# First attention of a two-layer network: three rounded products become one unrounded product, and the score tiles change their order

## The reference

```python
def _L0_xattn_ref(x, latents, ln_m_g, ln_m_b, ln_l_g, ln_l_b, Wq, Wkv, Wout):
    heads, dim_head = (16, 64)
    scale = dim_head ** (-0.5)
    x = layer_norm(x, ln_m_g, ln_m_b)
    lat = layer_norm(latents, ln_l_g, ln_l_b)
    q = lat @ Wq
    kv_input = jnp.concatenate([x, lat], axis=1)
    kv = kv_input @ Wkv
    k, v = jnp.split(kv, 2, axis=-1)
    ...
    dots = jnp.einsum('bhid,bhjd->bhij', q, k) * scale
    attn = jax.nn.softmax(dots, axis=-1)
    out = jnp.einsum('bhij,bhjd->bhid', attn, v)
    out = out.transpose(0, 2, 1, 3).reshape(b, m, heads * dim_head)
    return out @ Wout
...
x = x + _L0_xattn_ref(ctx_1024, _layernorm(x, axis=-1), ...)
x = x + _L0_ffn_ref(_layernorm(x, axis=-1), ...)
x = x + _L1_xattn_ref(_layernorm(x, axis=-1), ctx_1024, ...)
x = x + _L1_ffn_ref(_layernorm(x, axis=-1), ...)
```

## Time and profile before

| | |
|---|---|
| median of 3 runs | 792.21 us (791.63 to 795.18) |
| span of the profiled execution, first to last instruction | 788.3 us; its own time isn't listed apart from the three |
| TensorE's clock as granted, mean | 0.948 |
| busy: PE, DVE, ACT, POOL | 706.3, 475.7, 378.0, 377.4 us |
| transfers | 50.62 MB |

### The profile page before, as it was taken

How to read it: one execution, slowest core, us unless ns; L and a number is a source line. 1 busy time by engine, 2 the same in 40 slices (tenths; PEclk the granted TensorE clock), 3 DMA queues, 4 the chain that set the end, 5 groups by cost and what they waited for, 6 DMA issues and landing times.

```text
span 788.3 us, 13872 instructions
## 1 busy us (share of the span) xinstructions
PE 706.3 (90%) x4810; PEld 430.8 (55%) x4810; DVE 475.7 (60%) x966; ACT 378.0 (48%) x580; POOL 377.4 (48%) x361
## 2 busy tenths in 40 slices
PE   4899999999999999999999999997995687568991
PEld 3654555545556555556545545566995343336661
DVE  4745484585585875667477478465443386845553
ACT  4475554564654554655445444344552643223440
POOL 7264453473464475444464553634333304674552
PEclk9999999999999999999999999998998697569996
DMA  9999999990000000000030004301212500122325
GB/s 253 197 201 197 204 190 10 4 4 1 1 1 2 1 14 1 1 1 1 1 121 2 1 1 108 114 24 32 72 32 80 155 1 28 35 75 69 88 66 177
DMA packets 109867, 50.62 MB, mean 64 GB/s; under 512 B 44804, under 2 KB 103048, under 8 KB 109800
## 3 DMA queue, kind: packets, MB, share of 16 engines
q1 hardware_dynamic: 106280, 42.46, 36.0%
q0 software_dynamic: 3520, 7.27, 2.7%
HBM read 20.07 MB, written 29.64 MB: 63 GB/s over the span
## 4 chain that ended last, share of the span: by engine, by line
PE 74%; DVE 11%; issue 5%; ACT 3%; POOL 3%; DMA 2%; another core or an unknown queue 1%; SPq 1%; DVEq 0%; POOLq 0%; ACTq 0%
PE PSUM L1631 14%; PE PSUM L1663 13%; PE PSUM L1598 5%; PE PSUM L1463 5%; PE PSUM L1498 4%; PE PSUM L1468 4%; PE PSUM L1729 4%; PE PSUM L1423 3%; PE PSUM L1425 2%; PE PSUM L1424 2%; PE PSUM L1612 2%; PE PSUM L1605 2%; PE PSUM L1649 2%; PE PSUM L1693 2%; DVE REC L1377 1%
## 5 line engine op out<-in xcount | busy, mean ns | idle before, releaser
L866 ACT ACTIVATE PT<-PSUM 128x1024 f32<-128x1024 f32 x128 | 128.6, 1024 | 134.1 <-PE PSUM L1631 133.7
L690 POOL TENSOR_TENSOR PSUMS<-PT 128x1024 f32<-128x1024 f32 x32 | 76.0, 2376 | 210.4 <-ACT PT L866 171.4
L690 POOL TENSOR_TENSOR PSUMS<-PSUMS,PT 128x1024 f32<-128x1024 f32 x62 | 149.6, 2413 | 16.8 <-ACT PT L866 9.9
L1254 DVE TENSOR_REDUCE TOPS<-PSUM 128x2 f32<-128x1024 f32 x128 | 152.1, 1220 | 6.9 <-PE PSUM L1598 6.5
L1663 PE MATMUL PSUM<-PT,BIG 128*64 128x512 f32 x512 | 130.6, 611 | 0.0
L1209 DVE TENSOR_TENSOR SIL<-SIL,PSUM 128x256 f32<-128x256 f32 (+1 forms) x62 | 32.2, 519 | 65.7 <-ACT SIL L783 46.8
L1244 DVE TENSOR_TENSOR KL<-PSUM,KH 128x512 fp32r<-128x512 f32 x32 | 22.1, 691 | 68.2 <-ACT KH L844 67.7
L1598 PE MATMUL PSUM<-KH,QH 64*128 64x512 f32 x256 | 57.9, 449 | 4.0 <-DVE QL L1247 3.7
L1663 PEld LDWEIGHTS PSUM<-PT,BIG 128*64 128x64 f32 x512 | 28.4, 135 | 53.4 <-issue 52.0
L1598 PEld LDWEIGHTS PSUM<-KH,QH 64*128 64x128 f32 x256 | 24.2, 183 | 59.2 <-DVE TOPS L1254 24.9
L783 ACT ACTIVATE SIL<-PSUM 128x256 f32<-128x256 f32 (+1 forms) x62 | 28.6, 462 | 56.7 <-PE PSUM L1463 31.4
(11 more groups left out here) (256 smaller groups left out, 1365.5 us busy)
## 6 DMA issues: line engine op xcount, KB each, us to landing
lists_d<-EMPTY SPq DMA_DIRECT2D x3, 2730.0 KB, 35.3
lists_b<-EMPTY SPq DMA_DIRECT2D x3, 2470.0 KB, 33.4
lists_d<-EMPTY SPq DMA_DIRECT2D x1, 2665.0 KB, 34.9
XG<-lists_d SPq DMA_DIRECT2D x39, 65.0 KB
lists_b<-EMPTY SPq DMA_DIRECT2D x1, 2405.0 KB, 17.2
BIG<-in_L_ffn_w SPq DMA_DIRECT2D x1, 2048.0 KB
W2ALL<-in_L_ffn_w SPq DMA_DIRECT2D x4, 512.0 KB, 6.2
PT<-results_d SPq DMA_DIRECT2D x8, 256.0 KB, 4.4
```

The lines of the kernel that those rows point to most:

```text
L690: pool.tensor_tensor(PSUMS[:, i % 2], PTT[:, i % 2, 0] if kt == 1 else PSUMS[:, i % 2], PTT[:, i % 2, kt], ALU.add).then_inc(s_ps, 1)
L866: act.activation(PTT[:, i % 2, kt], PSUM[:, place:place + 2, :], ACT.Exp, scale=DH ** -0.5).then_inc(s_exp, 1)
L1254: dve.tensor_reduce(TOPS[:, c, 0, :], PSUM[:, place:place + 2, :], AX.X, ALU.max).then_inc(s_max, 1)
```

## The change

Queries, keys, values and the context's keys are made by one unrounded product each, straight from the loaded weights WA and unsplit features XF; the context's values from WA alone. A score tile has two steps in place of four: unrounded KF by QF, then the rounded minus ones by TOPROW. The maxima tiles stay rounded. ScalarE rounds the queries (QH) and copies them (QF); VectorE rounds the keys (KH) and copies them (KF). Queries and keys have semaphores of their own (`s_qp`, `s_kp`), and their two banks are released one by one (`s_qf`, `s_kf`). The splitting of weights, features and context goes. WA and XF get memory of their own. In ITERATION the score tiles s1 and s2 move forward, and D behind t2. The load of the first experts' gates is cut at expert 3, whose place QF holds until the last score tile.

```diff
-        WA = PT[:, 0:2, :, :].rearrange("p a k n -> p (a k n)")[:, 0:3 * INNER]
...
-            WH = sb1("WH", 3, INNER)
-            WL = sb1("WL", 3, INNER)
-
-            XTH = sb1("XTH", 2, S)
-            XTL = sb1("XTL", 2, S)
-
-            QH = sb1("QH", 2, S)
-            QL = sb1("QL", 2, S)
-            KH = sb1("KH", 2, S)
-            KL = sb1("KL", 2, S)
+            def sb1(name, *shape, dt=F32):
+                return first.enter_context(nc.sbuf_tensor(name, [P, *shape], dt))
+
+            WA = sb1("WA", 3, INNER)
+            XF = sb1("XF", 2, S)
+
+            QH = sb1("QH", 2, S, dt=F32R)
+            KH = sb1("KH", 2, S, dt=F32R)
+            KF = sb1("KF", 2, S)
...
-            "E A B PC CA0 C CA1 O0 ADD CS V qk p0 p1 t0 s0 t1 p2 t2 D s1 t3 p3 t4 P0 P2 s2 s3 rows mt O1 OUT "
+            "E A B PC CA0 C CA1 O0 ADD CS V qk p0 p1 t0 s0 t1 p2 s1 t2 D p3 s2 t3 t4 P0 P2 s3 rows mt O1 OUT "
...
-            gates_of(0, E - 1)
+            gates_of(0, GROUP - 1)
+            gates_of(GROUP, E - 1)
 
             sp.wait_ge(s_sc, len(scored))
+            gates_of(GROUP - 1, GROUP)
...
-            round_weights(1, ld_wk)
-            act.wait_ge(*CTD.at(0, "ct"))
-            act.activation(CTH[:, :], CT, ACT.Copy).then_inc(s_cth, 1)
-            round_weights(0, ld_wq)
...
-                    act.wait_ge(s_qk, a + 1)
+                    act.wait_ge(s_qp, a + 1)
                     if a >= 2:
 
-                        act.wait_ge(s_sc, scores_of(a - 2))
-                    act.activation(QH[:, a % 2, :], PSUM[:, place, :], ACT.Copy).then_inc(s_qkh, 1)
-                    act.activation(KH[:, a % 2, :], PSUM[:, place + 1, :], ACT.Copy).then_inc(s_qkh, 1)
+                        act.wait_ge(s_top, TOPS_OF * (a - 1))
+                    act.activation(QH[:, a % 2, :], PSUM[:, place, :], ACT.Copy).then_inc(s_qh, 1)
                     if a >= GROUP:
                         act.wait_ge(s_sc, context_of(a // GROUP - 1))
-                    act.activation(QF[:, a % GROUP, :], PSUM[:, place, :], ACT.Copy).then_inc(s_qkh, 1)
+                    act.activation(QF[:, a % GROUP, :], PSUM[:, place, :], ACT.Copy).then_inc(s_qf, 1)
...
-            rest_of_weights(1, 1)
-            dve.wait_ge(s_cth, 1)
-            dve.wait_ge(*CTD.at(0, "ct"))
-            dve.tensor_tensor(CTL[:, :], CT, CTH[:, :].bitcast(F32), ALU.subtract).then_inc(CTD.sem, 1)
-            rest_of_weights(0, 2)
...
-                    dve.wait_ge(s_qkh, 3 * a + 2)
-                    dve.tensor_tensor(KL[:, a % 2, :], PSUM[:, place + 1, :], KH[:, a % 2, :].bitcast(F32),
-                                      ALU.subtract).then_inc(s_qkl, 1)
-                    dve.wait_ge(s_qkh, 3 * a + 3)
-                    dve.tensor_tensor(QL[:, a % 2, :], PSUM[:, place, :], QH[:, a % 2, :].bitcast(F32), ALU.subtract).then_inc(s_qkl, 1)
+                    dve.wait_ge(s_kp, a + 1)
+                    if a >= 2:
+
+                        dve.wait_ge(s_sc, scores_of(a - 2))
+                    dve.tensor_copy(KH[:, a % 2, :], PSUM[:, place + 1, :]).then_inc(s_kh, 1)
+                    dve.tensor_copy(KF[:, a % 2, :], PSUM[:, place + 1, :]).then_inc(s_kf, 1)
...
-            def three(dst, aH, aL, bH, bL):
-                pe.matmul(dst, aH, bH, start=True, stop=False)
-                pe.matmul(dst, aH, bL, start=False, stop=False)
-                return pe.matmul(dst, aL, bH, start=False, stop=True)
...
-                    last = three(PSUM[:, 7 - part, pr % GROUP * P:(pr % GROUP + 1) * P], WH[:, 1, c], WL[:, 1, c], CTH[:, :], CTL[:, :])
+                    last = pe.matmul(PSUM[:, 7 - part, pr % GROUP * P:(pr % GROUP + 1) * P], WA[:, 1, c], CT, start=True, stop=True)
...
-                        last = three(PSUM[:, place + n, :], XTH[:, k, cols], XTL[:, k, cols], WH[:, 2, c], WL[:, 2, c])
+                        last = pe.matmul(PSUM[:, place + n, :], XF[:, k, cols], WA[:, 2, n * BANK:(n + 1) * BANK], start=True, stop=True)
...
-                        for step, weights in enumerate((WH, WL)):
-                            for p in range(GROUP):
-                                last = pe.matmul(
-                                    PSUM[p * M:(p + 1) * M, place + b // 2, b % 2 * 2 * P:(b % 2 + 1) * 2 * P].rearrange("p (g n) -> p g n", g=2),
-                                    CT[:, ctx_b], weights[:, 2, :].bitcast(F32).rearrange("p (g q n) -> p g q n", g=2, q=GROUP)[:, :, p, :],
-                                    start=step == 0, stop=step == 1)
+                        for p in range(GROUP):
+                            last = pe.matmul(
+                                PSUM[p * M:(p + 1) * M, place + b // 2, b % 2 * 2 * P:(b % 2 + 1) * 2 * P].rearrange("p (g n) -> p g n", g=2),
+                                CT[:, ctx_b], WA[:, 2, :].rearrange("p (g q n) -> p g q n", g=2, q=GROUP)[:, :, p, :],
+                                start=True, stop=True)
...
-                    for w in range(2):
-                        last = three(PSUM[:, place + w, :], WH[:, w, c], WL[:, w, c], XTH[:, k, :], XTL[:, k, :])
-                    last.then_inc(s_qk, 1)
-                    release(mine, (s_qkl, 2 * a + 2))
+                        pe.wait_ge(ld_wq, 16)
+                    for w, made in enumerate((s_qp, s_kp)):
+                        pe.matmul(PSUM[:, place + w, :], WA[:, w, c], XF[:, k, :], start=True, stop=True).then_inc(made, 1)
+                    release(mine[0:1], (s_qf, a + 1))
+                    release(mine[1:2], (s_kf, a + 1))
...
-                        pe.wait_ge(s_qkl, 2 * i + 2)
+                        pe.wait_ge(s_qf, i + 1)
+                        pe.wait_ge(s_kf, i + 1)
                         if i == 0:
                             pe.wait_ge(s_const_r, 1)
-                    for step in range(4):
-                        if (kt, step) == (0, 3):
+                    for step in range(2):
+                        if (kt, step) == (0, 1):
                             pe.wait_ge(s_toprow, i + 1)
                         for h in range(2):
                             r = slice(DH * h, DH * h + DH)
                             c = slice(kt * P, (kt + 1) * P)
-                            lhs = (KH[r, k, c], KL[r, k, c], KH[r, k, c], MINUS[r, :])[step]
-                            rhs = (QH[r, k, :], QH[r, k, :], QL[r, k, :], TOPROW[r, i % GROUP, :])[step]
-                            last = pe.matmul(PSUM[:, place + h, :], lhs, rhs, start=step == 0, stop=step == 3)
+                            lhs = (KF[r, k, c], MINUS[r, :])[step]
+                            rhs = (QF[r, i % GROUP, :], TOPROW[r, i % GROUP, :])[step]
+                            last = pe.matmul(PSUM[:, place + h, :], lhs, rhs, start=step == 0, stop=step == 1)
```

More of the change, by code:

```diff
@@ L259, in build @@
         s_tr = sem("lane_turned")
[L260 to L264, removed]
+        CTD = Steps(sem("ctx_dve"), ["ct", "raw"])
+        s_xf = sem("features")
         s_const_r = sem("rounded_consts")
@@ L269, in build @@
         s_vp, s_v = sem("values"), sem("values_kept")
-        s_qk, s_qkh, s_qkl = sem("queries_keys"), sem("qk_high"), sem("qk_low")
+        s_qp, s_kp = sem("queries"), sem("keys")
+        s_qh, s_qf, s_kh, s_kf = sem("queries_rounded"), sem("queries_kept"), sem("keys_rounded"), sem("keys_kept")
         s_top, s_max, s_comb = sem("top_scores"), sem("half_max"), sem("row_max")
@@ L517, in sync_program @@
             sp.dma_start(W1U.rearrange("p (e n) -> p e n", e=E), w1[:, :, F_B:].rearrange("e p n -> p e n")).then_inc(ld_w1, 16)
-            sp.wait_ge(s_qk, ALL)
+            sp.wait_ge(s_kp, ALL)
             sp.wait_ge(s_vp, B * KT)
@@ L768, in keep_weights @@
                 if j == 0:
-                    act.wait_ge(ld_w1, 48)
+                    act.wait_ge(ld_w1, 80)
                 if j >= 2:
@@ L859, in scalar_program @@
                         act.wait_ge(s_ps, 3 * (i - 1))
-                    if i < 2 and kt == 0:
-                        act.wait_ge(s_wl, 3)
                     if i == 1 and kt == 0:
@@ L954, in features @@
                 dve.wait_ge(s_gk, 1)
-                if b > 0:
-                    dve.wait_ge(s_xth, b)
-                    dve.wait_ge(*XTD.at(b - 1, "low"))
-                if b > 2:
-                    dve.wait_ge(*RP0.at(b - 3, "logits"))
-                dve.tensor_scalar(XT[:, :], PSUM[:, bank, :], GAINS[:, 0:1], GAINS[:, 1:2], ALU.mult, ALU.add).then_inc(XTD.sem, 1)
-            def split_features(b):
-                k = b % 2
-                dve.wait_ge(s_xth, b + 1)
-                dve.wait_ge(*XTD.at(b, "feat"))
-                dve.tensor_tensor(XTL[:, k, :], XT[:, :], XTH[:, k, :].bitcast(F32), ALU.subtract).then_inc(XTD.sem, 1)
+                if b >= 2:
+                    dve.wait_ge(s_kp, (b - 1) * PAIRS)
+                    dve.wait_ge(s_vp, (b - 1) * KT)
```

(13 more changed lines are left out.)

48 lines of the change are left out of this document (8 added, 40 removed).

## The result

The changed kernel takes 857.0 us (median of 4 runs, 856.41 to 859.27); the kernel before, beside it on the same chip, 791.9. The ratio is 1.0816, 95% interval 1.0783 to 1.0848. The forecast was 853, slower.

A forecast was written before the change was run, and what follows sets the result against it. The prediction took TensorE, busy 119.25 of 120 us at full clock, to bound the kernel. Its terms, 37 + 21 + 4 + 3 - 4 = +61, gave span 849 and time 853 us; 8 in 10 within 828 to 876.

The forecast's parts named there:

- The exchange of products: On TensorE, one unrounded product (0.86 us) for three rounded (0.695): 224 exchanges at 0.165 more, +37 us.
- the start: Before the first projection: rounding of features and rests go, context's values are halved; -4 us, between -2 and -6.
- Rivals C: Score tiles: unrounded products on the two row halves queue, 110 us more, 963 us; chance 0.04.
- D (763): Rival on TensorE: an unrounded product costs only 0.46 us, 53 us fewer in place of 37 more; chance 0.02.
- the prediction's A: Rival at score tile s3: the same-pair wait is hidden, 832 us; chance 0.15.
- E: Rival for the whole kernel: gains and losses meet within 0.5% (4 us), 792 us; chance 0.02.
- The change of format: On TensorE, passing between unrounded and rounded products: taken as 0, upper bound 19 us.
- Rival B: On TensorE: each change of number format costs 0.1 us, 869 us in all; chance 0.15.
- The same-pair wait and D: s3 or first spread waits 0.7 us for s2's PSUM pair, 31 times, +21; normalising step on ScalarE, +4 us.
- rival A: Of the experiments: the wait is not the order's, or would stand elsewhere without it; 850 to 857 us.
- The copies of the keys: At t0, TensorE waits for VectorE's late key copies: five waits, +0.65 us each, +3 us.
- The expert stages: After the attention: expected to take as long as before.

The follow-up runs named there:

- e1: The changed kernel with the old written order of an iteration put back; 824.9 us, ratio 1.0353.
- e6: The kernel before with only the score tiles made by unrounded products, projections and old order kept; 816.5 us, ratio 1.0248.
- e2: The kernel before with the new written order of an iteration alone, its rounded products kept; 820.4 us, ratio 1.0499.
- e7: The changed kernel with row-maxima tile t3 moved ahead of score tile s2 and nothing else; ratio 1.0644.
- e0: The changed kernel measured again, as it is, on another chip; 846.0 us, ratio 1.0841.
- e3: The changed kernel with the start of the inverse of the context sums queued on VectorE behind the copies of the keys; ratio 1.0714.

## Why the prediction was right, and where it was off

Time and side were right, 853 against 857, and the mechanism too. That it came so near is in part luck: by the sizes below, products, wait and D were taken 7 too large together, and 8.6 of spacing and waits for PLACE and 3.5 behind the marker weren't forecast.

**The exchange of products** was forecast +37. In the old order the table gives 19.1 for the score tiles (e1), 15.1 for projections and values and 1.1 for the turning ahead of them, 35.3; 0.9 of it belongs to the first projections, where rounded products stand 0.43 apart and not 0.23 (from start to start of what follows, 15.98 - 12.40 = 3.58 for 18.07 - 15.34 = 2.73), which the prediction put under the start. So 34.4 for 37. Its unit, 0.86 for an unrounded product and for a pair on two row halves, was right (1.09 = 0.86 + 0.23). The small excess came from taking every rounded product at 0.2315, while the first behind another shape or the short t4 took more: s2 and s3 stand 1.18 now, and stood 153.88 - 152.85 = 1.03 and 1.02 before, 0.15 and 0.16 less. Rivals C (963) and D (763) fell with the tile's 1.09; the prediction's A (the wait hidden, 832) fell with the 31 waits, and E with the measured difference. The Trainium skill's page "TensorE: Matmul & The Clock Gate" (section "Wait — 56ns, not 53.3ns?") gives 215.7 ns from start to start at 512 columns; the rounded products here stand 231 apart. By its figure this term would have been an estimated +48; no run here comes near it.

**The change of format** was forecast at nothing, and costs nothing that shows (e6). Rival B is out at its 0.1; a smaller price would be hidden in the sum of pair and maxima step.

**The same-pair wait and D** were forecast 21 + 4. There are 31 waits, as counted, 20.8 us in all: 22 of 0.58 to 0.63, six of 1.02 or 1.03 in the iterations with D, one of 0.79, two of 0.17. D is thus 6 x 0.39 = 2.3 in place of 4, and the pair 18.5 in place of 21. The forecast's 1.60 - 0.92 = 0.68 took t4 at 0.46; behind a tile of its own shape it takes 0.51, which leaves the 0.63. In the two of 0.17 another wait, for PLACE, had covered it. e2 shows the order as the sole cause, e7 the pair; rival A is out by both.

**The copies of the keys** were forecast +3. TensorE waited 8.5 us nine times at t0; before it was 4.4. This is +4.1. The five iterations with context sums were foreseen; e1, which has five waits and 5.5, shows that the other four come with the new order, and VectorE is late in them too.

**Not forecast at all:** the two waits for PLACE, +2.5, and the spacing of the new order, 7.8 - 2.3 and 0.6 in projections and turning, +6.1, of which 1.7 is the lowered clock behind 437 us. The prediction priced each item of the new order by the row of the item and not by what stands ahead of it: s1 and s2 now follow a value product directly, and s3 has t4 ahead of it and the sums behind it (the listings under e1).

**The start** was forecast -4, 0.9 for the first projections included. The waits ahead of 20 us went from 4.5 to 2.1, the context's keys and values from 8.5 to 5.8, and the first projections cost 0.9 more: -4.2.

**The expert stages** were to stay as long as before. They are 3.5 longer, 269.0 against 265.5, and as much in e0, by the median spans of that chip: 844.2 - 585.4 = 258.8 against 778.1 - 522.8 = 255.3. Right behind the marker TensorE waits for gathered rows, waits from 586 to 670 us:

```profile
PE PSUM L1385 <- DMA XG<-lists_b: 4.0, 2, 2.4
```

There it was 0.2 before. What delays the gather was not tried and stays open, and so does whether the 3.5 is the change's at all: the kernel before ran between 787.2 and 797.1 on one chip, its marker was profiled on one chip only, and by the same reckoning e1's part behind the marker is not longer on its chip (823.1 - 553.4 = 269.7 against 794.1 - 522.8 = 271.3).

**A plain iteration** was to take 13.2. From one projection to the next, 40.87 to 54.59, it takes 13.72 with a wait of 1.02, or 13.33 with one of 0.63.

Sum of what was measured ahead of the marker: 34.4 for the products, 6.1 spacing, 20.5 for the exponential, 4.1 for the copies, 2.5 for PLACE, -4.2 for the start, together 63.4; the marker moved by 62.8, and the 0.6 between them is in the small items. With 3.5 behind it, 66.3, the growth of the span from 788.3 to 854.6.

## What to carry to other kernels

When buffers turn in a ring and the items in an order are moved, write down for each item which earlier item held its buffer, and compare the work that lies between with the time of the reader; a move can bring the two nearest together though no item grew. Price an item by its distance to the next in the order it will have, the change of shape ahead of it included. And a step moved out of the way of one reader on a busy engine is put in the way of the next: the same move took 4 us of waits from one kernel and added 4 to another.

## What the runs showed of the hardware that had not been expected

Short idle stretches can cost more than themselves, and not each time. In e2 TensorE's granted clock went down to 1.2 GHz for about 3.4 us three times, twice behind waits of 0.63 and 1.11 or 1.12 us within 3 us, once behind 1.43 and 0.16; in the changed kernel once, behind 1.24 and 0.17. In e2 that took 5.1 us in all, on top of the waits themselves. But the clock stayed at 1.00 behind 0.63 and 1.12 at 87 us and behind 1.43 and 0.16 at 425 us in e2, behind 1.24 and 0.17 at 295 us in the changed kernel, behind both such places in e3, and behind single waits of 1.98 (e7) and 2.19 (e3). So the waits alone don't decide it, and what does stays open. A new order that makes only short waits can cost 38 us where its waits are 28.5.
